# A conditioned residual network with paged attention: the pages of values fetched by the sync engine instead of by indirect gathers

## The reference, cut to what matters

```
x = x + L0(x)                            # per-sequence 32x32 mix
x = x + L1(x)                            # linear layer plus per-sequence adapter
# L2: attention
q, k = rope(rmsnorm(x @ Wq)), rope(rmsnorm(x @ Wk));  v = x @ Wv
kc = k_cache[block_table]                # (64, 16 pages, 32 tokens, 8, 128)
vc = v_cache[block_table]                # the same pages, of values
scores = q @ concat(kc, k) * SCALE, masked;  probs = softmax(scores)
x = x + (probs @ concat(vc, v)) @ Wo
x = x + L3(x)                            # per-sequence 32x32 mix
```

## Time and profile before

| what | value |
|---|---|
| median of three runs | 2390.04 us (2388.29 to 2393.2) |
| the profiled execution, its own time | 2394.14 us |
| span of its profile | 2392.4 us |
| granted TensorE clock, mean | 0.994 |
| PE busy | 2312.0 us, 97% of the span |
| PE weight loads | 2010.2 us, 84% |
| DVE busy | 1760.8 us, 74% |
| ACT busy | 1535.2 us, 64% |
| POOL busy | 1395.5 us, 58% |
| HBM | 374.53 MB read, 79.69 MB written |

### The profile page before, as it was taken

One profiled execution on the slowest core, in us unless ns is written; L12 is line 12 of the kernel. 1 busy time (PEld: TensorE's weight loads), 2 busy tenths in 40 slices (PEclk: granted clock), 3 DMA queues, 4 the chain that ended last, 5 costly groups with the idle time before them and its releaser, 6 DMA issues.

```text
span 2392.4 us, 58277 instructions
## 1 busy us (share of the span) xinstructions
PE 2312.0 (97%) x15392; PEld 2010.2 (84%) x15392; DVE 1760.8 (74%) x5422; ACT 1535.2 (64%) x4221; POOL 1395.5 (58%) x2249
## 2 busy tenths in 40 slices
PE   8999999999998899999999999999999999998999
PEld 5778888888887788888888888888888888887777
DVE  4434777777778887887887887887887887886232
ACT  4324666666667777777777777777777777775221
POOL 1003454444447777877877877877877877872000
PEclk9999999999998999999999999999999999999999
DMA  4335333333337777777767777777767777775332
GB/s 164 95 110 163 102 98 102 111 106 102 97 115 257 221 224 239 253 228 237 255 223 241 253 228 237 255 223 242 252 220 245 253 223 241 253 221 194 110 132 101
DMA packets 347959, 455.96 MB, mean 191 GB/s; under 512 B 34506, under 2 KB 280842, under 8 KB 343695
## 3 DMA queue, kind: packets, MB, share of 16 engines
q1 hardware_dynamic: 308398, 315.83, 41.9%
q0 software_dynamic: 36864, 134.23, 16.9%
q10 hardware_dynamic: 2528, 4.29, 0.5%
HBM read 374.53 MB, written 79.69 MB: 190 GB/s over the span
## 4 chain that ended last, share of the span: by engine, by line
PE 48%; DVE 23%; issue 19%; ACT 5%; POOL 3%; DMA 1%; DVEq 0%; ACTq 0%; POOLq 0%; SPq 0%
PE S L1168 11%; PE oP L1168 11%; DVE regC L987 8%; PE S L1260 7%; DVE k_lo L284 7%; PE oP L1241 3%; PE oP L1092 3%; DVE regC L986 3%; PE S L1209 3%; PE bank L1092 2%; PE oP L1122 2%; ACT regC L721 2%; PE bank L1260 2%; DVE nmx L975 1%; DVE rinv L981 1%
## 5 line engine op out<-in xcount | busy, mean ns | idle before, releaser
L1241 PE MATMUL oP<-regC,regK 128*128 128x128 f32 x4096 | 541.2, 275 | 0.1
L1241 PEld LDWEIGHTS oP<-regC,regK 128*128 128x128 f32 x4096 | 507.2, 192 | 9.6 <-issue 0.3
L975 DVE CUSTOM_DVE_ANT_0 regC<-S,mask 128x544 f32<-128x544 f32 x512 | 368.1, 719 | 187.9 <-issue 185.7
L715 ACT CAST k_hi<-regK 128x544 fp32r<-128x544 f32 x512 | 331.3, 647 | 210.5 <-PE S L1209 184.1
L721 ACT ACTIVATE regC<-regC,nmx 128x544 f32<-128x544 f32 x512 | 384.9, 752 | 58.8 <-DVE nmx L975 49.8
L534 POOL TENSOR_TENSOR regC<-regC 128x256 f32<-128x256 f32 x320 | 244.3, 784 | 278.3 <-DVE regC L944 278.3
L549 POOL TENSOR_TENSOR q_hi<-regC,ones 128x128 fp32r<-128x128 f32 x512 | 262.3, 512 | 233.8 <-PE S L1209 229.1
L1092 PE MATMUL bank<-ident,regC 128*128 128x128 f32 x2048 | 321.1, 279 | 26.9 <-ACT regC L765 21.0
L284 POOL TENSOR_TENSOR k_lo<-regK,k_hi 128x192 fp32r<-128x192 f32 x512 | 341.4, 667 | 3.3 <-ACT k_hi L715 3.3
L987 DVE TENSOR_SCALAR regC<-regC,rinv 128x512 f32<-128x512 f32 x512 | 337.8, 660 | 0.0
L284 DVE TENSOR_TENSOR k_lo<-regK,k_hi 128x352 fp32r<-128x352 f32 x512 | 328.2, 641 | 2.9 <-ACT k_hi L715 2.9
(11 more groups left out here) (137 smaller groups left out, 4468.9 us busy)
## 6 DMA issues: line engine op xcount, KB each, us to landing
regK<-kT_cache SPq DMA_DIRECT2D x1024, 128.0 KB
qkT_d<-regC SPq DMA_DIRECT2D x160, 256.0 KB, 2.3
regC<-qkT_d SPq DMA_DIRECT2D x64, 512.0 KB
oT_d<-regC SPq DMA_DIRECT2D x64, 256.0 KB
regK<-oT_d SPq DMA_DIRECT2D x16, 1024.0 KB, 5.0
regC<-wqk SPq DMA_DIRECT2D x10, 1024.0 KB, 5.2
v_d<-regC SPq DMA_DIRECT2D x32, 256.0 KB, 2.3
regK<-qkT_d SPq DMA_DIRECT2D x64, 128.0 KB
```

The costliest lines, as they stand in the source:

```text
L715: nc.scalar.copy(k_hi[u % 2].rearrange("p (s t) -> p s t", t=PSIZE), k_sb[b][:, :, h, :]).then_inc(s_khi, 1)
L975: nc.vector.tensor_tensor_reduce(out=p_sb[u % 4], in0=scores, in1=mask[u // HK % 2][:], scale=-SCALE, scalar=3e38, op0=ALU.add, op1=ALU.mi ...
L1241: last = nc.tensor.matmul(oP[:, j * 512:j * 512 + P], v_sb[b][:, m, u % HK * D:(u % HK + 1) * D], pT_sb[u % 2][:, m * P:(m + 1) * P], star ...
```

## The change

The indirect gathers go, with the table of row numbers, its copies, its input and its semaphores. SP keeps the registers in which it read the page numbers for the keys and issues 16 more DMAs per sequence from them, each one page of values: 32 rows of 4 KB into a quarter of the partitions. They stand after the wait for `s_po` and ahead of the own values. For sequence 0 they follow its key pages, ahead of the first `store_qk`; for sequence 1 they follow its own values, ahead of the load of `wo`. PE's wait for the values counts 256 for each sequence instead of 64.

```
@@ block.sync
             def load_pages(b, par, first=0, count=NPP):
                 ...
+                return pages
+
+            def load_v_pages(pages, par, first=0):
+                for n in range(first, first + len(pages)):
+                    sp.dma_start(v_sb[par][n % 4 * PSIZE:(n % 4 + 1) * PSIZE, n // 4, :],
+                                 v_cache[bass.ds(pages[n - first], 1)].rearrange("a t n -> (a t) n")).then_inc(s_v[par], 16)
...
-            load_pages(0, 0)
+            load_v_pages(load_pages(0, 0), 0)
...
-                    load_pages(1, 1, (t - 4) * 2, 2)
+                    pages1.append(load_pages(1, 1, (t - 4) * 2, 2))
             load_own(1, 1)
             load_own_v(1, 1)
+            for i in range(8):
+                load_v_pages(pages1[i], 1, i * 2)
...
                         sp.wait_ge(s_klo, g * UG + HK * (k + 1))
-                        load_pages(b, k % 2)
+                        pages = load_pages(b, k % 2)
                         sp.wait_ge(s_po, g * (2 * BT) + 2 * (k + 1))
+                        load_v_pages(pages, k % 2)
                         load_own_v(b, k % 2)
@@ block.gpsimd
-                k, m = (u - 10) // HK, (u - 10) % HK
-                if m < 4 and not (fixed and not 2 <= g * BT + k + 2 < B):
-                    if m == 0:
-                        b = g * BT + (k + 2)
-                        pool.wait_ge(s_idx, b + 1)
-                        pool.wait_ge(s_po, g * (2 * BT) + 2 * (k + 1))
-                        next_idx(b + 1, (k + 3) % 4)
-                    gather_v((k + 2) % 4, k % 2, m)
@@ block.tensor
-                    pe.wait_ge(s_v[b], pair * 64 + 64)
+                    pe.wait_ge(s_v[b], pair * VLOAD + VLOAD)
@@ inputs
-        "v_cache": np.asarray(L2_cond_v_cache).reshape(PAGES * PSIZE, HK * D),
+        "v_cache": np.asarray(L2_cond_v_cache).reshape(PAGES, PSIZE, HK * D),
```

More of the change, by code:

```diff
@@ L70, in ge, with build @@
         eng.wait_ge(sem, val)
-def build(nc, x, cond_row, id_row, bt_row, idx_pages, seq_tok, seq_all, w0, w3, wb, bias,
+def build(nc, x, cond_row, id_row, bt_row, seq_tok, seq_all, w0, w3, wb, bias,
           lora_a, lora_b, wqk, wv, wo, qn, kn, kT_cache, v_cache, ident_c, iota_c, row_c, invf_c,
@@ L170, in build @@
         invf, seqi = qr_sb[0][:, 3 * P:3 * P + D // 2], qr_sb[0][:, 3 * P + D // 2:4 * P].bitcast(I32)
-        idxi = qr_sb[1][:, 0:B * 4].bitcast(I32)
         at[0] = 0
@@ L203, in build @@
         ang, turns, red = (regK[:, KV + (i + 4) * NT * HD:KV + (i + 5) * NT * HD] for i in range(3))
-        idx_all = sb("idx_all", [P, (B + 1) * 4], I32)
-        idx = [sb(f"idx{i}", [P, 4], I32) for i in range(4)]
         cond = sb("cond", [1, B], I32)
@@ L247, in build @@
         s_ang, s_sin, s_tab, s_dve = sem("s_ang"), sem("s_sin"), sem("s_tab"), sem("s_dve")
-        s_idx0 = sem("s_idx0")
         s_w, s_whi, s_wlo = sem("s_w"), sem("s_whi"), sem("s_wlo")
@@ L257, in build @@
         s_wo_in, s_wohi, s_wolo = sem("s_wo_in"), sem("s_wohi"), sem("s_wolo")
-        s_idx = sem("s_idx")
         s_k = [sem(f"s_k{i}") for i in range(2)]
@@ L272, in build @@
         s_l3, s_out, s_outst = sem("s_l3"), sem("s_out"), sem("s_outst")
-        LATE = 16 * 10
+        LATE = 16 * 9
         KLOAD = 16 * (NPP + 2)
+        VLOAD = 16 * NPP
         block = ctx.enter_context(nc.Block())
@@ L334, in _ @@
             for dst, src in ((seqt[:], seq_tok), (invf, invf_c), (rowc[:], row_c), (qn_sb[:, 0, :], qn), (qn_sb[:, 1, :], kn),
-                             (btab[:], bt_row), (iota[:], iota_c), (seqi, seq_all), (idxi, idx_pages), (w3_sb[:], w3)):
+                             (btab[:], bt_row), (iota[:], iota_c), (seqi, seq_all), (w3_sb[:], w3)):
                 sp.dma_start(dst, src).then_inc(s_late, 16)
@@ L391, in _ @@
                 store_qk(QKB - 2, t)
+            pages1 = []
             for t in range(NT):
@@ L504, in _ @@
                     pick(i, j)
[L506 to L516, removed]
             nc.gpsimd.memset(ones[:], 1.0).then_inc(s_ones, 1)
             pool.wait_ge(s_ones, 5)
[L520 to L526, removed]
             def add_halves(e, t):
@@ L578, in _ @@
                 step(0, u)
-                if 2 <= u < 6:
-                    gather_v(1, 1, u - 2)
             with pool.Fori(0, NT - 1) as g:
@@ L920, in _ @@
             nc.vector.tensor_copy(seqf[:], seqi)
-            nc.vector.memset(idx_all[:, B * 4:], 0.0)
-            nc.vector.tensor_scalar(idx_all[:, 0:B * 4], idxi, float(PSIZE), rowc[:], ALU.mult, ALU.add).then_inc(s_idx0, 1)
             dve.wait_ge(s_sin, 2)
@@ L1361 @@
         "bt_row": bt.reshape(1, B * NPP),
-        "idx_pages": np.repeat(bt.reshape(B, 4, 4).transpose(2, 0, 1).reshape(4, B * 4), PSIZE, axis=0),
         "seq_tok": seq.reshape(NT, BT)[:, of_row].T,
```

## The result

| | before | changed |
|---|---|---|
| median, us | 2389.59 (4 runs) | 2602.79 (4 runs, 2600.15 to 2605.81) |
| span of the profiled execution, us | 2392.4 | 2601.8 |
| mean granted TensorE clock | 0.994 | 0.958 |

The ratio is 1.089, with a 95% interval from 1.0871 to 1.0909. The forecast was 2595 us in a range from 2507 to 2748.

What follows compares the result with a forecast made beforehand. PE bounds the kernel before, POOL close behind; after the change SP's own issuing sets the turn. 2394.1 + 199.6 (61 turns) + 6 (start of projections) - 5 (end) = 2595 us, +8.4%, range 2507 to 2748.

Steps and rivals of the forecast that it cites:

- The bound: Attention loop: SP works 18.9 of 22.67 us per turn; with the new DMAs 25.9, so 61 turns grow by 199.6 us.
- The price of an issue: SP's value pages in each turn: 0.44 us per DMA, 7.0 us per turn; from below 0.37, from above 0.54.
- a term that stood only in the low bound: Key pages on SP lose their hitches when no gather runs beside them: 0.2 us per turn, giving 2507 us.
- The start of the projections: SP's 16 value pages stand ahead of the first store, so ACT and PE stop: +6 us, bounds 4 and 12.
- The load of `wo`: Another 7 us of issuing ahead of it lie beside SP's 11.5 us rest: nothing, up to 3 us for the upper end.
- The end: Last sequence begins when its keys land, some 16.5 us after SP's last start instead of some 21.5: -5 us.
- The -10 in the low bound: Last term of the low bound, 2394.1 + 131 + 4 - 10 = 2519 us, where the forecast took -5 for the end.
- What is late next: Attention: key pages of the sequence after the next lose some 6 us in hand; engines then stop once per sequence.
- Rival A: DMA side binds: transfers into a quarter of the partitions drain slower than SP issues, 0.59 us each; 2741 us, chance 0.12.
- Rival B: Clock: each PE stop in short sequences brings 13.7 us at half clock, up to 80 us more; 2675 us, chance 0.13.
- Rival C: Faster: SP's issues, under 0.235 us each, fit its rest and POOL's relief gives 20.5 to 41 us; 2374 us, chance 0.04.
- Rival D: No change: SP's work is in part overlapped and the two effects cancel; 2394 us, chance 0.03.

Runs made afterwards that it cites:

- the narrow one: Changed kernel with the same 16 DMAs per sequence, each bringing 128 of 1024 columns, an eighth of the bytes: 2596.24 us, ratio 1.0868.
- the move: Changed kernel with sequence 0's value pages issued one by one among the stores of the last but one block of projections: 2596.14 us, ratio 1.0855.
- the cheaper version: Changed kernel with SP reading the 16 page numbers without the check of their bounds: 2364.69 us, ratio 0.9894.
- the four pages: Kernel before with three gathers left on POOL and the last quarter of a sequence's values as 4 pages on SP: 2373.72 us, ratio 0.993.
- the kernel before with the cheaper reading: Kernel before, gathers kept, with SP reading page numbers without the bounds check: 2391.34 us, ratio 1.0003.

## Why the prediction was right, point by point

- **The bound**: SP works 18.9 us of 22.67 in a turn and has 3.77 us free. This is what carried the forecast. A turn with 16 DMAs more was put at 25.9 us and measured 26.08; the growth of the 61 turns was put at 199.6 us and measured 207.7.
- **The price of an issue**: 0.44 us was forecast, (7.30 - 0.37) / 15 = 0.46 measured. The move of 29 ns is there, the register arithmetic isn't, as told. The DMA itself has a median of 370 ns and not the 322 of the own values. Neither its size nor its 4 KB rows explain that, since the narrow one takes 370 too. Added up over SP's timelines, the value pages took 7.56 us a turn from the first start to the last end, and 0.18 us to get there, where 7.0 was forecast: 43 us too little over 61 turns. The rest of SP's turn, put at no change, became 0.6 us shorter, 35 us over all turns. Half of that is in the 16 key pages (8.30 us, against 8.61), a term that stood only in the low bound. The two errors leave 8 us. That the total came so near is in part luck, since each of them was four to five times as large.
- **The start of the projections**: +6 forecast; the attention began 5.3 us later, and the move gave 6.7 back.
- **The load of `wo`**: nothing forecast. SP's rest of 11.5 us before its first turn is down to 2.3 us, and nothing else is seen of it.
- **The end**: -5 forecast, -3.6 measured, of which only 1.2 lie in the attention. The step said that the last sequence begins as soon as its keys land, 16.5 us after SP's last start where it was 21.5. The traces bear the mechanism out and not the sizes: ACT's first split of the last sequence comes 17.2 us after that start (2361.93, behind a wait for key pages), and came after 19.6 before (2151.31). That is 2.4 us instead of 5, and its eight splits then took 1.2 us longer. The other 2.4 us lie behind the attention, where nothing was forecast; why is open. The -10 in the low bound had no working of its own.
- **What is late next**: the key pages. It is what POOL and ACT wait for, though not once per sequence, as told, but 41 times in 62; the value pages have no wait in the list.
- **Rival A** fell with the narrow pages. The rule of the Trainium skill (SBUF — State Buffer, Door 1: The DMA port swizzle) that such a transfer reaches half of the ports may hold: 3.3 us to landing, against 2.2 for a key page of the same size, though the two differ in the length of their rows and in their place in the queue as well. But it never held SP.
- **Rival B** happened, and cost nothing. The mean clock between 754 and 2345 us was 0.94, against 1.00:

```profile
754.10:2344.70 1590.60, 1390.42 (x10665) 1281.09 (x10666) 1171.28 (x3593) 1037.18 (x2227) 745.06 (x1473) 0.94 0.75 209
```

  One stop of PE, with the 4.03 us in which it stood before this row:

```profile
1455.28 1.09 PE L1067 MATMUL bank<-ident,regC 128*128 128x128 f32 x4 [4.03 <-ACT regC L742]
```

  The granted clock is 1.00 until 1455 us, 0.60 in the microsecond in which PE starts again, 0.50 (the 1.2 GHz level) from 1456 to 1458, 0.69 in the next microsecond and 1.00 again from 1459. That is some 3 us at the lower level, where the rival had 13.7. And it cost nothing: if PE had set the turn, SP would have waited for POOL's splits behind it, but SP's waits inside the 61 turns are 0.6 us. PE ran slower inside a gap that it had anyway. In the cheaper version the stops are gone and the clock is at 1.00:

```profile
760.00:2100.00 1340.00, 1308.48 (x10472) 1200.48 (x10471) 1164.90 (x3522) 1023.57 (x2184) 721.63 (x1445) 1.00 0.87 243
```

- **Rival C** had the right price and not the right condition. POOL's relief is worth 22.6 us, inside the 20.5 to 41 that it was given, though with all gathers gone most of it reached PE by way of ACT, which the rival didn't name. I asked for an issue under 0.235 us; the other way to it is less other work on SP, and that is the version which beats both kernels.
- **Rival D** fell: the kernel is 8.9% slower, and SP's rest is spent before anything is lost, as the four pages show.
- **The rule** of the Trainium skill (DMA: Bandwidth & Descriptors, Issuing engines are not separate DMA queues), that issuing is usually small beside the DMA itself, misleads here. An issue of 0.46 us is small beside the 3.3 us until a page has landed, but landings overlap, and issues on one engine add up: without the 16 issues per turn the kernel took 2367.77 us instead of 2602.79, while an eighth of the bytes changed 0.3%.

## What to carry to other kernels

An engine that only issues DMAs shows no busy time, so its load has to be added up from its timeline: issues, register reads and waits over one turn of the loop. Its rest per turn, divided by the price of one issue, says how many DMAs may be moved to it. Take the rest against what the other engines will need after the move, not before it: here 22.21 us, not 22.67. At 22.0 us of work SP cost nothing, and at 22.6 it was already the bound. If it is over, look first for the work on it that has nothing to do with transfers: here 4.0 us of checks per turn decided between 9% slower and 1% faster.

## What the hardware showed that I had not expected

- The time that SP spends on an issue doesn't depend on the bytes: 370 ns at the median with 32 rows of 4 KB and with 32 rows of 512 bytes. But own values, also 32 rows on the same queue, took 316 to 322, and key pages with 128 rows 333.
- Reading a number from a table into a register with its bounds check costs 0.147 + 0.018 us and gaps, 0.25 us in all, and without it hardly anything beyond the one load of 0.97 us for 16 numbers (from the queries to the first key page 1.64 us in all).
- Turning back at the end of SP's loop took long: from 1484.26 to 1488.41 us, where other turns follow within 0.65 us, with no wait recorded for it. Over all turns, and counted from the end of the last DMA, it took 3.0 us on the average, against 0.26 elsewhere. It is in every sum above. It isn't a fixed price: in the kernel before with the cheaper reading, which has the fewest instructions in this loop, 7.9 of the 8.5 us there are a recorded wait, so only 0.6 are left. That is part of why SP's rest grew by 5.0 us a turn there, and not by 4.0. What causes it wasn't tested.
